# Small loads once and in order of use, scales from a diagonal of the parameters, h behind the first t, the last chunk in two halves

## What is computed

```
# layer 0: the first 2048 rows are users, the other 3072 are items
u = par_u[0] * par_u[1] * (diag_u[:, None] * x_u @ W_u) + x_u
i = par_i[0] * par_i[1] * (diag_i[:, None] * x_i @ W_i) + x_i
e = concatenate([u, i])
t = adj.T @ e
h = adj @ t
x1 = layernorm(x + (layernorm(h) * gamma + beta + x))
# layer 1
dinv = rsqrt(adj.sum(axis=0) + 1)
z = dinv[:, None] * (x1 @ W)
x2 = layernorm(x1 + relu(dinv[:, None] * (adj.T @ z + z) + b))
```

## Time and profile before

| | us |
|---|---|
| median of 3 runs | 635.2 (634.48 to 636.16) |
| profiled execution | 634.37 |
| its span, first to last instruction | 632.7 |
| TensorE busy | 596.1 (94%) |
| VectorE busy | 336.9 (53%) |
| ScalarE busy | 135.5 (21%) |
| GpSimd busy | 108.6 (17%) |
| read from memory | 202.82 MB, 323 GB/s over the span |

### The profile page before, as it was taken

How to read it: one execution, slowest core, us unless ns; L and a number is a source line. 1 busy time by engine, 2 the same in 40 slices (tenths; PEclk the granted TensorE clock), 3 DMA queues, 4 the chain that set the end, 5 groups by cost and what they waited for, 6 DMA issues and landing times.

```text
span 632.7 us, 10807 instructions
## 1 busy us (share of the span) xinstructions
PE 596.1 (94%) x4780; PEld 232.5 (37%) x4780; DVE 336.9 (53%) x427; ACT 135.5 (21%) x197; POOL 108.6 (17%) x126
## 2 busy tenths in 40 slices
PE   4997999999999999999999999999999999979775
PEld 3633333333333333333333344554433434213112
DVE  0789757876867777886776784465130402103004
ACT  1114151241506033150604127212000100001001
POOL 3004233060704213050503204100000000000000
PEclk8999999999999999999999999999999999999998
DMA  7998597978789695978879497599999999999992
GB/s 238 387 366 301 183 389 248 391 255 299 261 293 347 206 389 205 351 253 299 295 261 386 164 390 265 188 349 409 409 410 410 410 410 410 411 409 409 410 398 89
DMA packets 86003, 204.83 MB, mean 324 GB/s; under 512 B 4539, under 2 KB 7099, under 8 KB 85957
## 3 DMA queue, kind: packets, MB, share of 16 engines
q1 hardware_dynamic: 83888, 202.75, 85.9%
q10 hardware_dynamic: 2068, 1.40, 0.7%
HBM read 202.82 MB, written 1.31 MB: 323 GB/s over the span
## 4 chain that ended last, share of the span: by engine, by line
PE 83%; DMA 13%; DVE 3%; ACTq 0%; issue 0%; ACT 0%; DVEq 0%
PE psum L765 33%; PE psum L874 22%; PE psum L965 14%; PE psum L882 6%; DMA slot<-in_adj_dram 5%; DMA turned<-in_adj_dram 3%; DMA last_slot<-in_adj_dram 3%; PE psum L759 2%; PE psum L804 2%; DMA par<-in_L_gnn_par_i_dram 1%; PE psum L985 1%; PE psum L945 1%; PE psum L933 1%; DVE slot L594 1%; PE psum L826 1%; PE psum L982 1%
## 5 line engine op out<-in xcount | busy, mean ns | idle before, releaser
L594 DVE STREAM_TRANSPOSE slot<-slot 128x2048 f32<-128x2048 f32 x80 | 177.9, 2280 | 72.0 <-PE psum L765 71.9
L765 PE MATMUL psum<-slot,E 128*64 128x512 f32 x768 | 171.9, 596 | 0.3 <-DVE slot L600 0.2
L874 PE MATMUL psum<-slot,T 32*64 32x512 f32 x2560 | 142.4, 590 | 3.5 <-DVE slot L594 3.5
L365 POOL COPY turned<-last_slot 32x1024 f32<-32x1024 f32 x80 | 84.6, 1058 | 281.0 <-DVE last_slot L594 276.6
L965 PE MATMUL psum<-slot,E 128*64 128x512 f32 x512 | 115.0, 596 | 10.5 <-DMA slot<-in_adj_dram 9.8
L419 ACT ACTIVATE turned<-last_slot 32x1024 f32<-32x1024 f32 x80 | 84.3, 1054 | 45.0 <-DVE last_slot L594 43.3
L765 PEld LDWEIGHTS psum<-slot,E 128*64 128x64 f32 x768 | 52.4, 137 | 108.1 <-issue 107.2
L874 PEld LDWEIGHTS psum<-slot,T 32*64 32x64 f32 x2560 | 55.2, 132 | 88.7 <-issue 86.4
L706 DVE TENSOR_TENSOR T<-psum,dinv 128x256 f32<-128x256 f32 x10 | 4.3, 425 | 145.8 <-PE psum L985 145.3
L410 ACT ACTIVATE T<-T 32x256 f32<-32x256 f32 x60 | 24.8, 414 | 210.7 <-DVE T L578 209.4
L965 PEld LDWEIGHTS psum<-slot,E 128*64 128x64 f32 x512 | 35.0, 137 | 86.7 <-issue 60.4
(11 more groups left out here) (106 smaller groups left out, 273.7 us busy)
## 6 DMA issues: line engine op xcount, KB each, us to landing
slot<-in_adj_dram SPq DMA_DIRECT2D x152, 1024.0 KB, 14.6
last_slot<-in_adj_dram SPq DMA_DIRECT2D x30, 1024.0 KB, 7.6
turned<-in_adj_dram SPq DMA_DIRECT2D x10, 1024.0 KB, 16.2
X<-in_x_dram SPq DMA_DIRECT2D x5, 256.0 KB, 5.9
out_dram<-T ACTq DMA_DIRECT2D x10, 128.0 KB, 5.9
T<-in_L_gnn_W_u_dram ACTq DMA_DIRECT2D x2, 16.0 KB, 4.8
T<-in_L_gnn_W_i_dram ACTq DMA_DIRECT2D x2, 16.0 KB, 10.2
beta_b<-in_L_gnn_ln_beta_dram SPq DMA_DIRECT2D x1, 32.0 KB, 8.3
```

Source lines behind the costliest of these rows:

```text
L365: nc.gpsimd.tensor_copy(turned[c * Q32:(c + 1) * Q32, a].rearrange("p h k j r -> p (h k j) r"), last_blocks[a * Q32:(a + 1) * Q32, :, c, : ...
L594: v.transpose(parts, parts).then_inc(chunk_cut, 1)
L765: return mm(acc[half[b % 2], :], E[:, b, :], view[:, b % CB, :], start=(b < 2), stop=(b >= NB - 2))
L874: last = mm(acc[half[h], a, :], T[step % 2][rows_a, jb, d, :], slot[step % 2][rows_a, h:NF:2, :, cols], start=step == 0 and jb == 0 and d ...
```

## The change

- ScalarE's short loads come in another order, without the wait for the memsets: W_u, par_u, par_i, diag_u, diag_i, W_i. The weights are loaded once each, into 64 rows of an unused part of the same tile (`W_raw`); VectorE writes both centred copies from there. The parameters go to one row for each row of `diag` (4 and 6), no longer to 128.
- VectorE multiplies the two parameters, and scales a 10 x 10 corner of the identity by them (`par_diag`). TensorE multiplies `diag` by this diagonal, in place of the transpose, and VectorE only copies the result.
- VectorE centres W_i behind the first group of E. Before, both weights were centred ahead of everything.
- Step 0 follows the order of the others: eight cuts ahead of the copies of t, h directly behind the turn of t, and ten pairs of sums in each of the two places.
- The last chunk of all is loaded as two transfers of two rows a partition, and the sweep waits for the second (`tail_loaded`) ahead of its third matmul pair.

```diff
@@ sync
-                    if (k, m) >= TAIL:
+                    if (k, m) == (TAIL[0], RES * NQ - 1):
+                        q, J = tail_part(m)
+                        for to, b, half_landed in ((view[:, 0:WB], 0, landed), (view[:, WB:CB], WB, tail_loaded)):
+                            sp.dma_start(to, adj_rows[:, q, b:b + WB, J * JW:(J + 1) * JW]).then_inc(half_landed, 16)
+                    elif (k, m) >= TAIL:
                         load(view, landed, *tail_part(m))
@@ scalar
-            act.dma_start(diag[0:USERS // CB, :], diag_u.rearrange("(q j) -> q j", j=JW)).then_inc(scales_loaded, 16)
-            act.dma_start(diag[USERS // CB:NQ, :], diag_i.rearrange("(q j) -> q j", j=JW)).then_inc(scales_loaded, 16)
-            act.wait_ge(weights_zeroed, 3)
-            load_w(0, WM[:, 0, :], W_u)
-            act.dma_start(par[:, 0:2], par_u.unsqueeze(0).to_broadcast([P, 2])).then_inc(scales_loaded, 16)
-            act.dma_start(par[:, 2:4], par_i.unsqueeze(0).to_broadcast([P, 2])).then_inc(scales_loaded, 16)
-            load_w(1, WM[:, 2, :], W_i)
+            users = USERS // CB
+            act.dma_start(W_raw[:, 0, :], W_u).then_inc(weights_loaded[0], 16)
+            act.dma_start(par[0:users, :], par_u.unsqueeze(0).to_broadcast([users, 2])).then_inc(scales_loaded, 16)
+            act.dma_start(par[users:NQ, :], par_i.unsqueeze(0).to_broadcast([NQ - users, 2]))\
+               .then_inc(scales_loaded, 16)
+            act.dma_start(diag[0:users, :], diag_u.rearrange("(q j) -> q j", j=JW)).then_inc(diag_loaded, 16)
+            act.dma_start(diag[users:NQ, :], diag_i.rearrange("(q j) -> q j", j=JW)).then_inc(diag_loaded, 16)
+            act.dma_start(W_raw[:, 1, :], W_i).then_inc(weights_loaded[1], 16)
@@ vector
-            for i in range(2):
-                dve.wait_ge(weights_loaded[i], 16 * 2)
+            def centre_weights(i):
+
+                dve.wait_ge(weights_loaded[i], 16)
...
+                dve.wait_ge(weights_zeroed, 2)
                 for h in half:
-                    v.tensor_scalar(WM[h, 2 * i, h], WM[h, 2 * i, h], mean_w[h, i:i + 1], None, ALU.add)\
+                    v.tensor_scalar(WM[h, 2 * i, h], W_raw[:, i, :], mean_w[half[0], i:i + 1], None, ALU.add)\
                      .then_inc(weights_centred, 1)
...
-            dve.wait_ge(scales_loaded, 16 * 4)
-            link(v.tensor_tensor(par2[:, 0:1], par[:, 0:1], par[:, 1:2], ALU.mult))
-            link(v.tensor_tensor(par2[:, 1:2], par[:, 2:3], par[:, 3:4], ALU.mult))
+            centre_weights(0)
+            dve.wait_ge(scales_loaded, 16 * 2)
+            link(v.tensor_tensor(par2[:, :], par[:, 0:1], par[:, 1:2], ALU.mult))
+            dve.wait_ge(ident_ready, 1)
+            v.tensor_scalar(par_diag[:, :], ident[0:NQ, 0:NQ], par2[:, 0:1], None, ALU.mult).then_inc(par_ready, 1)
             dve.wait_ge(diagT_done, 1)
-            users = USERS // CB
-            link(v.tensor_scalar(by_row[0][:, :, 0:users], scale_turn[:, :, 0:users], par2[:, 0:1], None, ALU.mult))
-            link(v.tensor_scalar(by_row[0][:, :, users:NQ], scale_turn[:, :, users:NQ], par2[:, 1:2], None, ALU.mult))
+            link(v.tensor_copy(by_row[0], scale_turn))
...
+                if g == 0:
+                    centre_weights(1)
...
-                early = NF - 2 if step == 0 else NF
-                for q in range(early):
+                for q in range(NF):
                     cut_chunk(step * NQ + q)
                 copy_tT(step)
                 copy_t(step, step % 2)
-                for q in range(early, NQ):
+                for q in range(NF, NQ):
                     cut_chunk(step * NQ + q)
@@ tensor
-            pe.wait_ge(scales_loaded, 16 * 4)
+            pe.wait_ge(diag_loaded, 16 * 2)
+            pe.wait_ge(par_ready, 1)
             for k in range(CB):
-                last = nc.tensor.transpose(scale_turn[:, k, :], diag[:, k::CB], ident[0:NQ, 0:NQ])
+                last = mm(scale_turn[:, k, :], diag[:, k::CB], par_diag[:, :], start=True, stop=True)
...
-                if step == 0:
-                    t_pairs(1, 0, 4)
...
-                if step == 0:
-                    t_pairs(1, 4, 14)
-                elif not final:
+                if not final:
                     t_pairs(step + 1, 0, HS // 2)
...
-                t_pairs(step + 1, 14 if step == 0 else HS // 2, HS)
+                t_pairs(step + 1, HS // 2, HS)
...
+                    if b == NB - WB and J == NJ - 1:
+                        pe.wait_ge(tail_loaded, 16)
```

More of the change, by code:

```diff
@@ L62, in build @@
         WB = CB // RES
+        half = [slice(0, F), slice(F, 2 * F)]
         X = sb("X", [P, NB, F])
@@ L76, in build @@
         WM = before[:, 256:256 + 3 * P].rearrange("p (w n) -> p w n", n=P)
+        W_raw = before[half[0], 256 + 3 * P:256 + 4 * P].rearrange("p (w f) -> p w f", f=F)
         W_out = sb("W_out", [P, P])
@@ L97, in build @@
         bias_b = sb("bias_b", [P, F])
-        par = sb("par", [P, 4])
-        par2 = sb("par2", [P, 2])
+        par = sb("par", [NQ, 2])
+        par2 = sb("par2", [NQ, 1])
+        par_diag = sb("par_diag", [NQ, NQ])
         scale = sb("scale", [P, NB])
@@ L119, in build @@
         acc = psum[:, 0:4, :]
-        half = [slice(0, F), slice(F, 2 * F)]
         t_acc = bank[5]
@@ L136, in build @@
         scales_loaded = sem("scales_loaded")
+        diag_loaded = sem("diag_loaded")
         weights_loaded = [sem(f"weights_loaded{i}") for i in range(3)]
@@ L146, in build @@
         turned_loaded = [sem(f"turned_loaded{i}") for i in range(2)]
+        tail_loaded = sem("tail_loaded")
         restored = sem("restored")
@@ L161, in build @@
         ones_ready = sem("ones_ready")
+        par_ready = sem("par_ready")
         diagT_done = sem("diagT_done")
@@ L268, in load_x @@
                              x_rows[:, q:q + GB // CB, :]).then_inc(x_loaded[g], 16)
-            load_x(0)
-            for g in range(1, NG):
+            for g in range(NG):
                 load_x(g)
@@ L538, in _ @@
             v = nc.vector
-            for i in range(2):
-                dve.wait_ge(weights_loaded[i], 16 * 2)
-                link(v.tensor_reduce(mean_w[:, i:i + 1], WM[:, 2 * i, :], AX, ALU.add))
-                link(v.tensor_scalar(mean_w[:, i:i + 1], mean_w[:, i:i + 1], -1.0 / F, None, ALU.mult))
+            def centre_weights(i):
+                dve.wait_ge(weights_loaded[i], 16)
+                link(v.tensor_reduce(mean_w[half[0], i:i + 1], W_raw[:, i, :], AX, ALU.add))
+                link(v.tensor_scalar(mean_w[half[0], i:i + 1], mean_w[half[0], i:i + 1], -1.0 / F, None, ALU.mult))
+                dve.wait_ge(weights_zeroed, 2)
                 for h in half:
-                    v.tensor_scalar(WM[h, 2 * i, h], WM[h, 2 * i, h], mean_w[h, i:i + 1], None, ALU.add)\
+                    v.tensor_scalar(WM[h, 2 * i, h], W_raw[:, i, :], mean_w[half[0], i:i + 1], None, ALU.add)\
                      .then_inc(weights_centred, 1)
-            dve.wait_ge(scales_loaded, 16 * 4)
-            link(v.tensor_tensor(par2[:, 0:1], par[:, 0:1], par[:, 1:2], ALU.mult))
-            link(v.tensor_tensor(par2[:, 1:2], par[:, 2:3], par[:, 3:4], ALU.mult))
+            centre_weights(0)
[3 more added lines that the diff above has]
+            v.tensor_scalar(par_diag[:, :], ident[0:NQ, 0:NQ], par2[:, 0:1], None, ALU.mult).then_inc(par_ready, 1)
             dve.wait_ge(diagT_done, 1)
-            users = USERS // CB
-            link(v.tensor_scalar(by_row[0][:, :, 0:users], scale_turn[:, :, 0:users], par2[:, 0:1], None, ALU.mult))
-            link(v.tensor_scalar(by_row[0][:, :, users:NQ], scale_turn[:, :, users:NQ], par2[:, 1:2], None, ALU.mult))
+            link(v.tensor_copy(by_row[0], scale_turn))
             for g in range(NG):
```

3 lines of the change are left out of this document (removed).

## The result

| | before | changed |
|---|---|---|
| median of 7 runs, us | 636.16 (634.48 to 637.45) | 633.13 (631.19 to 633.75) |
| profiled execution, us | 634.37 | 633.35 |
| its span, us | 632.7 | 631.6 |

The ratio is 0.9955, 95% interval 0.9939 to 0.9972: faster by 0.45%, some 2.9 us, where I had forecast 7.5 us and a range that ended at 631.7. Seven runs of before, four more than I had, put its median at 636.16, 1 us above the one I forecast from. The error is in the gain, not in the base.

What follows compares the result with a forecast made beforehand. TensorE was taken as the bound (83% of the span, 13% waiting for transfers). Opening 8.0 us, order 0.3 lost, tail 0, summed as 7.5: 634.37 to 626.9, stated as 627.7 against the median; range 625.3 to 631.7.

Steps and rivals of the forecast that it cites:

- The loads: Opening: 148 rows instead of 522, W_u at 4.5 us, diag at 6; chunks or short loads late had chance 0.16.
- W_i no wait: Opening: W_i lands by about 10 us, so its centring costs nothing; rival that it lands late, 637.7 us, chance 0.04.
- chunk 9: Opening: the tenth chunk lands at 36 us, bounds 33.7 and 40.4; at 40.4 the gain is 4.0 us, 631.2.
- The cuts: First t: VectorE cuts eight chunks in a row, 2.21 us each, 17.7 in all, and ends after TensorE's sums.
- The worth of the order in instructions: Step 0: the new order alone loses 0.3 us; old start of h, credited with work done ahead, is 48.59.
- The tail: Last chunk in two halves: TensorE waits for neither, gain 0 us.
- The clock that falls in the new wait: Rival, wait before the turn of t: TensorE's clock falls, 2.5 to 3 us lost, 630.5 us, chance 0.14.
- h at 41.1: First block: h starts at 41.1 us, 2.45 behind the end of the cuts at 38.6; gain 7.5 us.
- the four scale products start at 6.2 and take 0.65, as the transposes of diag did: Opening, TensorE: scale products start at 6.2 us and take 0.65, so the first projection starts at 6.9 instead of 13.29.
- so I drop 1.75 and give back 0.3 for a low clock that may last longer: Opening: five projections take 12.65 us instead of 14.10, as TensorE hardly waits in front of the first.
- microseconds won in the opening stay won at the end: Whole kernel: the last pass's load stream moves with TensorE, so the opening's gain stays if later stages keep their distances.
- the opening's part of the gain: Opening: the last E is done at 20.9 us, was 28.75; put at 8.0 us of the gain.

Runs made afterwards that it cites:

- order_only: The kernel before with only the new order of step 0; loads, scales and tail as before: 637.46 us, ratio 1.0023.
- plain_transposes: The changed kernel with diag turned by plain transposes against the identity, the two parameters left out of the scales: 631.94 us, ratio 0.9926.
- project_first: The changed kernel with the first projection of x ahead of the four scale products on TensorE: 631.95 us, ratio 0.9933.
- sums_ahead: combined with odd blocks' t in another bank, two pairs of block 1's sums and seven zero matmuls before the first turn of t: 628.13 us, ratio 0.9876.
- combined: project_first plus chunk 0 cut ahead of the last E and loads of beta, bias, gamma and W behind block 1's chunks: 630.22 us, ratio 0.9919.
- after: The changed kernel itself, with the full change against the kernel before: 633.13 us, ratio 0.9955.
- one_load: The changed kernel with the last chunk loaded in one transfer instead of two: 634.22 us, ratio 0.9971.
- loads_only: The changed kernel with the old order of step 0 and the last chunk in one load: 632.33 us, ratio 0.9942.
- filled_wait: The changed kernel with 17 matmuls of zeros in TensorE's wait before the first turn of t: 631.07 us, ratio 0.9933.
- before_filled: The kernel before with 16 matmuls of zeros in its wait for the two late cuts of step 0: 634.74 us, ratio 0.9978.
- first_and_filled: The changed kernel with the first projection ahead of the scale products and 17 zero matmuls before the first turn of t: 630.03 us, ratio 0.9913.
- combined_filled: combined with 15 matmuls of zeros before the first turn of t: 629.84 us, ratio 0.9903.

## Why the prediction was wrong

**Right.** The loads: W_u at 3.8 (forecast 4.5), start of the scale products 6.42 (6.2), W_i no wait, chunk 9 at 36.6 (36). The cuts: 17.57 us (17.7), and VectorE as the one that sets h. The worth of the order in instructions: 48.64 for a credited 48.59 in order_only (forecast 0.3 later). The tail: 0. The clock that falls in the new wait stood among the rivals, with its price a little high (2.5 to 3 us; 2.1 by the traces) and its chance too small.

**Wrong, with its size.** The prediction put h at 41.1; it started at 45.84 and its first half took 1.3 us longer. Against its steps:

- "the four scale products start at 6.2 and take 0.65, as the transposes of diag did": 2.03 us. A float32 product is eight records of 0.25 us here, the transpose four, 0.65 in all (plain_transposes). 1.4 us late, mis-sized by taking the row of another operation without a bound. With diag 0.2 later, the first projection started at 8.45 instead of 6.9. (The 0.2 is of a good execution: diag_i landed at 6.38, and between 6.5 and 7.2 in the other four kernels with the same wait.)
- "so I drop 1.75 and give back 0.3 for a low clock that may last longer": the projections took 23.67 - 8.45 = 15.2 us instead of 12.65, more even than the 14.10 of the kernel before. The low clock lasted until 14.5 us, so nothing was won back from it. This is the largest single term, 2.6 us. I had read 1.00 in the first microseconds as the full clock, where the matmuls of the same rows ran at half rate: eight transposes 1.91 us, which is 0.24 for a record against 0.11 later. With the first projection directly behind the transposes the term came out about as I had priced it in four profiles of six (1.97 us for the first projection in project_first, 1.73 for the second); sums_ahead shows some 2.5 and then full rate, combined 2.44 and 3.02. What failed is the premise that the engine "waits hardly at all in front of it": 0.35 us of waiting and 2.03 of products stood there, and the clock was low behind them. Which of the two keeps it low is open: plain_transposes has no products and was low, combined has no wait and fell.
- The clock in the wait: I gave it 0.14 as a rival. It fell in all four profiles with the whole wait of 4.1 us (after, order_only, plain_transposes, one_load), in combined with 2.51, and stayed up in project_first with 1.73; the old wait of 3.5 kept it in the kernel before and lost it in loads_only. It costs 0.86 in the turn and 1.3 in h (8.46 against 7.19 in filled_wait), 2.1 us. filled_wait shows the cause.
- "microseconds won in the opening stay won at the end": 1.46 us at the second h, 1.03 at the end (631.63 against 632.66); project_first 6.74 and 6.1. The lead is still 1.49 us where the last pass's first load goes out (399.56 against 401.05), so these tenths are lost behind it, in the pass whose pace the transfers set. Which transfer loses them is open.

In sum: diag 0.2, products 1.4, projections 2.6, from the end of the cuts to h 0.7 (3.18 us for 2.45; the slow turn less a shorter copy), first half of h 1.3, end 0.4, less 0.1 for the cuts: 6.5 us, which is what lies between the forecast for the profiled execution, 626.9, and 633.35. One figure in the prediction's sum is off by itself and changes nothing: the opening's part of the gain is 28.75 - 20.9 = 7.85, not 8.0.

**The comparison itself.** The trace of before was of a good execution: its clock stayed up in the late wait, while before_filled shows that the average one loses 1.4 us there. That fits a median of before 1.8 above its profiled execution, where that of the changed kernel is 0.2 below its own.

## What to carry to other kernels

A wait on TensorE can cost twice when work of full rate follows: once the wait, once the restart at half rate (2.1 us behind 4.1 us of waiting here, and 2.5 us of waiting already lost the clock once). Let work that needs no late load stand first: with the projection ahead of the scale products the first sums started at 16.6 to 18.8 us, with the products ahead of it at 18.6 to 20.6. Put useful matmuls into such a wait (another bank was all it took), or zeros, but no more than fit. Where one engine's chain (eight cuts) sets the next stage, shortening what stands ahead of it brings time one for one, until the next thing is late, here the landing of chunk 9. And a duration is taken from a row of the same operation, or bounded from both sides: a product is not a transpose.

## What the runs showed of the hardware that I had not expected

- The clock view reads 1.00 ahead of the first change that a trace holds, whatever the level is. Durations of equal matmuls tell: four transposes took 0.85 us at the low clock and 0.44 at the full one.
- The clock goes with much of these kernels' spread: project_first ran from 627.78 to 634.32 us with mean clocks from 0.998 to 0.990, filled_wait, whose late wait is closed, from 630.47 to 632.03. The mean clock does not rank runs by itself, for the reasons given above: the kernel before took 637.0 us with 0.995 and 634.67 with 0.990. The Trainium skill (TensorE: Matmul & The Clock Gate, What's actually happening) says that the monitor behind the clock does not start with the kernel, so that the same kernel sees a different number of slow matmuls from run to run. These runs agree: TensorE did the same in project_first and in the changed kernel until 5.4 us, and the clock rose at 5.4 in the one profile and at 14.5 in the other.
- A float32 product of 10 columns by a 10 x 10 matrix takes 0.245 us for each of its two records, at the low clock (2.03 us for eight) as at the full one (1.96).
- The clock can fall while TensorE reads busy: at 9.7 us in filled_wait (mean 0.93 in 8 to 10), behind a wait of 1.15 us and products from 7.21 to 9.24, and at 10.5 in combined, behind products from 8.51 to 10.47 and no wait at all. Four kernels with the same first projection and products as combined (project_first, first_and_filled, combined_filled, sums_ahead) kept it, so whether the products have a part in it is open.
